# Two edge gathers: several groups summed in one PSUM run, longer rings of places and hit matrices, tile steps further apart

## The reference, cut to what matters

```python
x = x + _L0_gnn_ref(_layernorm(x), W_r, W0_w, W0_b, edge_index, edge_type_16, 6250)
x = x + _L0_ffn_ref(_layernorm(x)[None], gate_w, gate_b, w1, b1, w2, b2)[0]   # 8 experts
x = x + _L1_gnn_ref(_layernorm(x), edge_index, L1_gnn_W, L1_gnn_b)
x = x + _L1_ffn_ref(_layernorm(x)[None], W_ih, W_hh, ...)[0]                   # LSTM

# inside the first:                                       # inside the third:
msg = h_all[edge_type, src] / deg[edge_type, dst][:, None]  # norm[:, None] * h[src]
agg = segment_sum(msg, dst, num_segments=N)                 # segment_sum(..., dst, N)
```

## Time and profile before

| | us |
|---|---|
| median of the executions timed without a profile | 4071.44 (4070.2 to 4076.07) |
| span of the profiled execution | 4443.8 |
| first gather, from POOL's first gather DMA to its last | 805.7 to 1981.6 |
| second gather, likewise | 2525.9 to 3672.7 |
| POOL: busy in L941, in L1676 | 755.1, 770.6 |

### The profile page before, as it was taken

One profiled execution on the slowest core, in us unless ns is written; L12 is line 12 of the kernel. 1 busy time (PEld: TensorE's weight loads), 2 busy tenths in 40 slices (PEclk: granted clock), 3 DMA queues, 4 the chain that ended last, 5 costly groups with the idle time before them and its releaser, 6 DMA issues. The chain is left out here.

```text
span 4443.8 us, 59668 instructions
## 1 busy us (share of the span) xinstructions
PE 3422.0 (77%) x18753; PEld 2613.4 (59%) x18753; DVE 1898.4 (43%) x5881; ACT 912.0 (21%) x2407; POOL 1686.3 (38%) x1769
## 2 busy tenths in 40 slices
PE   7999999455567666667999554566667779999996
PEld 3444444354556555565666444445555557999996
DVE  4555300133334444454555421223334445544687
ACT  2333333000000111112333200000000002444554
POOL 1000000566666666653222366666666660000000
PEclk9999999677777777778999766777888889999998
DMA  4333444333444545553333323333444444433333
GB/s 148 149 149 149 154 168 164 116 107 110 124 122 144 161 134 148 150 150 108 116 113 110 109 86 94 107 116 122 126 138 146 152 154 147 153 126 119 110 109 113
DMA packets 246926, 580.34 MB, mean 131 GB/s; under 512 B 45059, under 2 KB 130588, under 8 KB 232783
## 3 DMA queue, kind: packets, MB, share of 16 engines
q1 hardware_dynamic: 158816, 334.44, 21.9%
q0 software_dynamic: 85344, 238.92, 18.3%
q10 hardware_dynamic: 2448, 3.15, 0.2%
HBM read 384.29 MB, written 191.42 MB: 130 GB/s over the span
## 5 line engine op out<-in xcount | busy, mean ns | idle before, releaser
L1676 POOL DMA_INDIRECT b_msg<-scratch_gx,k_src_row x782 | 770.6, 985 | 385.2 <-issue 220.0
L941 POOL DMA_INDIRECT a_msg<-scratch_hrel,k_rel_row x782 | 755.1, 966 | 424.1 <-issue 214.8
L717 PE MATMUL r_psm<-k_w,r_xnT 128*128 128x512 f32 x1568 | 696.4, 599 | 10.4 <-ACT k_slab L681 9.5
L1019 PE MATMUL a_ps<-a_hit,a_msg 128*128 128x128 f32 x3128 | 556.5, 343 | 170.6 <-issue 112.9
L1727 PE MATMUL b_ps<-b_hit,b_msg 128*128 128x128 f32 x3128 | 481.2, 317 | 197.3 <-issue 117.9
L1019 PEld LDWEIGHTS a_ps<-a_hit,a_msg 128*128 128x128 f32 x3128 | 501.3, 248 | 209.6 <-issue 137.4
L1727 PEld LDWEIGHTS b_ps<-b_hit,b_msg 128*128 128x128 f32 x3128 | 462.8, 230 | 246.4 <-issue 148.4
L2130 PE MATMUL l_psg<-k_hall,k_whhT 128*128 128x125 f32 x4640 | 550.7, 277 | 5.2 <-DVE k_hall L2256 5.2
L2130 PEld LDWEIGHTS l_psg<-k_hall,k_whhT 128*128 128x128 f32 x4640 | 538.4, 193 | 5.7 <-DVE k_hall L2256 5.7
L717 PEld LDWEIGHTS r_psm<-k_w,r_xnT 128*128 128x128 f32 x1568 | 294.2, 192 | 356.0 <-issue 342.5
L1831 DVE TENSOR_TENSOR k_accT<-k_accT,b_ps 128x256 f32 x196 | 82.6, 422 | 654.2 <-remote 476.0
(11 more groups left out here) (290 smaller groups left out, 4200.4 us busy)
## 6 DMA issues: line engine op xcount, KB each, us to landing
l_xr<-scratch_xrow SPq DMA_DIRECT2D x146, 512.0 KB
scratch_hrel<-k_slab SPq DMA_DIRECT2D x50, 1024.0 KB
scratch_hrel<-r_hst SPq DMA_DIRECT2D x48, 1024.0 KB
scratch_xrow<-n_xs SPq DMA_DIRECT2D x50, 512.0 KB
a_typ<-scratch_typ SPq DMA_DIRECT2D x196, 96.0 KB
a_msg<-scratch_hrel,k_rel_row POOLq DMA_INDIRECT x782
b_msg<-scratch_gx,k_src_row POOLq DMA_INDIRECT x782
n_xb<-scratch_gx SPq DMA_DIRECT2D x48, 256.0 KB
```

Source lines behind the costliest of these rows:

```text
L717: mm = pe.matmul(psm[:, c % 4], xnT[:, u, kk], k.w[:, kk, c * 512:(c + 1) * 512], start=(kk == 0), stop=(kk == 1))
L941: pool.indirect_dma_start(msg[:, q, j], None, table, bass.IndirectOffsetOnAxis(ap=rows_of[:, g, j:j + 1].bitcast(U32), axis=0)).then_inc(s ...
L1019: mm = pe.matmul(ps[:, u, kk, 0:WIN], msg[:, g % SL, j, kk * P:(kk + 1) * P], hit[:, u, j], start=(j == 0), stop=(j == pieces(g)[-1]))
L1676: pool.indirect_dma_start(msg[:, q, j], None, rows_of, bass.IndirectOffsetOnAxis(ap=k.src_row[:, g, j:j + 1].bitcast(U32), axis=0)).then_i ...
```

## The change

1. `run_regions` cuts the groups into runs of 4, 3, 2 or 1, the longest whose expected targets span at most 112 of the 128 window columns: groups 0 to 83 in fours, 84 to 113 in threes, 114 to 169 in twos, 170 to 195 alone, in all 85 runs. All groups of a run get the base of its first group (`stage_edges`, three small copies on DVE). PE adds up a whole run in PSUM, and DVE adds it to `accT` once: 85 adds in place of 196 in each gather.
2. `hit` has 4 buffers (first gather) and 6 (second). The one-hot types have 4. The ring of places has 8 and 12, the latter with four of them in `k.slab`, which is free by then.
3. `hit` is built 2 groups ahead (first) and 4 ahead (second), in place of 1. `weigh` runs 3 ahead in place of 1.
4. Each place has one landing semaphore for its four DMAs in place of four. The matmul loop has pieces outside and halves inside.
5. Tiles begin 2 slots later, and their steps stand further apart: `project` 6 and 7 slots after the beginning in place of 3 and 4, and so on. The loop has 9 slots after the last tile has begun in place of 5 (14 in place of 10 in the first gather).

```diff
-                        pe.wait_ge(s_dv, 2)
+                        pe.wait_ge(s_dv, 2 + sum(1 for _, _, m in k.regions if m > 1))
...
+                for a, z, m in k.regions:
+                    if m > 1:
+                        run = base_f[:, a:z].rearrange("o (n m) -> o n m", m=m)
+                        link(v.tensor_copy(run[:, :, 1:m], run[:, :, 0:1].broadcast_to([1, (z - a) // m, m - 1])))
...
-    SL, XR, SR, XN = 7, 4, 16, 16
+    SL, XR, SR, XN = 8, 4, 16, 16
+    HB, HT = 4, 4
...
-            begin = [k.ready[t] if along else t for t in range(NT)]
+            begin = [k.ready[t] + 2 if along else t for t in range(NT)]
...
-            slots = range(begin[-1] + 11)
+            slots = range(begin[-1] + 15)
+            landed = lambda g: 16 * sum(len(pieces(h)) for h in range(g % SL, g + 1, SL))
...
                     if along:
-                        types(0)
-                        types(1)
+                        for g in range(5):
+                            types(g)
...
                     for g in slots:
-                        if along and g + 1 < NG:
-                            weigh(g + 1)
+                        if along and g + 3 < NG:
+                            weigh(g + 3)
...
-    SL, XR, XB = 7, 4, 6
+    SL, XR, XB = 12, 4, 6
+    HB = 6
...
-        msg = sb("b_msg", [P, SL, PER, D])
-        hit = sb("b_hit", [P, 2, PER, WIN])
+        low, high = k.slab[:].rearrange("p (s j d) -> p s j d", j=PER, d=D), sb("b_msg", [P, SL - 4, PER, D])
+        msg = lambda q, j: low[:, q, j] if q < 4 else high[:, q - 4, j]
+        hit = sb("b_hit", [P, HB, PER, WIN])
...
-            first = [k.ready[t] if along else t for t in range(NT)]
+            first = [k.ready[t] + 2 if along else t for t in range(NT)]
...
-            slots = range(first[-1] + 6)
+            slots = range(first[-1] + 10)
...
                     def sums(g):
-                        u = g % 2
+                        n = k.run_of[g]
+                        begins, closes = g in k.leads, g + 1 in k.leads or g + 1 == NG
                         pe.wait_ge(s_p, g + 1)
-                        if g >= 2:
-                            pe.wait_ge(s_add, g - 1)
+                        if begins and n >= 2:
+                            pe.wait_ge(s_add, n - 1)
+                        pe.wait_ge(s_m[g % SL], landed(g))
                         for j in pieces(g):
-                            pe.wait_ge(s_m[g % SL][j], 16 * (g // SL + 1))
-                        for kk in range(2):
-                            for j in pieces(g):
-                                mm = pe.matmul(ps[:, u, kk, 0:WIN], msg[:, g % SL, j, kk * P:(kk + 1) * P],
-                                               hit[:, u, j], start=(j == 0), stop=(j == pieces(g)[-1]))
+                            for kk in range(2):
+                                mm = pe.matmul(ps[:, n % 2, kk, 0:WIN], msg(g % SL, j)[:, kk * P:(kk + 1) * P],
+                                               hit[:, g % HB, j], start=(begins and j == 0 and kk == 0),
+                                               stop=(closes and j == pieces(g)[-1]), skip_group_check=True)
                         mm.then_inc(s_mm, 1)
...
-                        for t in ahead(g, 2):
+                        for t in ahead(g, 3):
                             turn_own(t)
+                        for t in begun(g - 7):
+                            project(t, 1)
+                        for t in begun(g - 6):
+                            project(t, 0)
                         for t in begun(g - 4):
-                            project(t, 1)
-                        for t in begun(g - 3):
-                            project(t, 0)
-                        for t in begun(g - 2):
                             turn(t)
...
-                        if along and g + 1 < NG:
-                            build(g + 1)
+                        if along and g + 4 < NG:
+                            build(g + 4)
...
-                        if along and g < NG:
-                            add(g)
+                        if along and (g in k.leads[1:] or g == NG):
+                            add(g - 1)
```

More of the change, by code:

```diff
@@ L773, in stage_first @@
     s_t = (s_t0, s_t1)
-    s_m = [[k.pool_dma_sem(f"a_m{u}{j}") for j in range(PER)] for u in range(SL)]
+    s_m = [k.pool_dma_sem(f"a_m{u}") for u in range(SL)]
     nm = ("tok", "ld", "x0", "x1", "x2", "x3", "tp", "a", "st", "var", "std", "rec", "nm", "xn", "t2", "xt", "lg",
@@ L896, in sums @@
                         rest(k, pe, s_add, g + 1)
[L897 to L898 removed]
+                        rest(k, pe, s_m[q % SCAN], 16 * PER * (2 * i + q // SCAN + 1))
                         for kk in range(2):
                             for j in range(PER):
[L901 removed]
+                                mm = pe.matmul(ps[:, u, kk, 0:WIN], msg[:, q % SCAN, j, kk * P:(kk + 1) * P],
                                                hit[:, u, j], start=(j == 0), stop=(j == PER - 1))
@@ L1266, in _ @@
                     if along:
-                        hot(0)
-                        hot(1)
+                        for g in range(4):
+                            hot(g)
                         build(0)
+                        build(1)
                     v.wait_ge(S["tok"], 3)
@@ L1571, in stage_second @@
     pieces = lambda g: range(min(PER, -(-(k.E - g * EG) // P)))
-    s_m = [[k.pool_dma_sem(f"{name}m{u}{j}") for j in range(PER)] for u in range(SL)]
+    s_m = [k.pool_dma_sem(f"{name}m{u}") for u in range(SL)]
     halves = lambda a: a.rearrange("p (k c) -> p k c", k=2)
@@ L1823, in add @@
                     def add(g):
+                        n = k.run_of[g]
                         at = v.value_load(k.base[0:1, g:g + 1], min_val=0, max_val=k.NP - WIN)
                         v.wait_ge(s_mm, g + 1)
-                        if g:
-                            v.wait_ge(s_add, g)
-                        owned = sum(1 for t in range(NT) if max(first[t] - 1, 0) <= g)
+                        if n:
+                            v.wait_ge(s_add, n)
+                        owned = sum(1 for t in range(NT) if max(first[t] - 1, 0) <= g + 1)
                         if owned:
@@ L1874, in _ @@
                     if along:
-                        build(0)
+                        for g in range(4):
+                            build(g)
                     for n in range(16):
@@ L2316, in stage_lstm, with run_regions @@
         nc.all_engine_barrier()
+def run_regions(k):
+    span = lambda g, m: k.N * (((g + m) * EG / k.E) ** 2 - (g * EG / k.E) ** 2)
+    sizes, g = [], 0
+    while g < k.NG:
+        m = max([1] + [m for m in range(2, LONGEST + 1) if g + m <= k.NG and span(g, m) <= WIN - 16])
+        sizes.append((g, m))
+        g += m
+    regions = []
+    for g, m in sizes:
+        if regions and regions[-1][2] == m:
+            regions[-1] = (regions[-1][0], g + m, m)
+        else:
+            regions.append((g, g + m, m))
+    return regions
 def gnn_moe_gcn_lstm(nc, x, src, dst, edge_type_16, L0_gnn_W_r, L0_gnn_W0_w, L0_gnn_W0_b, L0_ffn_gate_w,
@@ L2338, in gnn_moe_gcn_lstm @@
     assert k.C * k.L == k.NP and k.N % k.L == 0
-    k.settled = [max(0, int(k.N * (g * EG / k.E) ** 2) - WIN // 2) // P for g in range(k.NG)]
+    k.regions = run_regions(k)
+    k.leads = [g for a, z, m in k.regions for g in range(a, z, m)]
+    k.run_of = [sum(1 for a in k.leads if a <= g) - 1 for g in range(k.NG)]
+    lead = lambda g: k.leads[k.run_of[g]]
+    k.settled = [max(0, int(k.N * (lead(g) * EG / k.E) ** 2) - WIN // 2) // P for g in range(k.NG)]
     k.ready = [next((g for g in range(k.NG) if k.settled[g] > t), k.NG) for t in range(k.NT)]
```

193 lines of the change are left out of this document (97 added, 96 removed).

## The result

The changed kernel takes **4106.9 us** (median of 4 executions, 4099.76 to 4108.0), the kernel before beside it 4073.8 (4 executions, 4070.2 to 4076.1). The ratio is 1.0078 with a 95% interval of 1.0064 to 1.0093: slower by 33 us (0.8%), well outside the 8 us that can't be told from no change. The profiled execution of the changed kernel is its fastest one: it took 4099.8 us, 7 less than the median, so its trace can show some 25 of the 33 us. The forecast of 4066 and the range up to 4090 were both too low.

A forecast was written before the change was run, and what follows sets the result against it. POOL's issue of gather DMAs was taken as the bound. Terms of -20 (waits gained), +9.4, +1.0 and +4 (tails) and +0.7 (edge-stage copies) made -5 us on the 4071.4 median: 4066, range 3975 to 4090.

The forecast's parts named there:

- What bounds the kernel: In both gathers POOL's issue of 782 indirect DMAs, 1.259 us each, is the bound, with its waits on top.
- The runs without a profile have almost none of POOL's waits: In the gathers, POOL's 321 us of profiled waits for PE are mostly absent from timed runs; 24 us taken.
- W = S - 6: W: POOL's gather waits in unprofiled runs, at least 0; S: what other stages are shorter by there, 0 to 110 us.
- S = 30: Stages outside POOL's issuing taken as 30 us shorter without a profile, leaving 24 us of POOL's waits.
- Of W's 24 us I take 20 as gained: In the gathers, all parts of the change together remove 20 us of POOL's waits; bounds 0 and 321.
- Rival 1: Slower: no POOL waits to remove, later projections stick out behind the last DMA; price 15 us, 4087; chance 0.25.
- the tails: Work behind each gather's last DMA, from steps further apart: 9.4 + 1.0 us second gather, 4 us first; bounds 0 and 20.
- beside POOL: 0: In each gather, 111 fewer adds save 47 us of DVE, but this lies beside POOL, so 0 us.
- The second tail: Behind the second gather: 12 projections left in place of 7, 9.4 us, and one more `weighted`, 1.0 us.
- The first tail: Behind the first gather: one more tile begins after the last group, 4 us.
- Rival 3: Late PE signals are in timed runs too; larger rings remove 138 us and half of 183: 3857; chance 0.08.
- What would show it: Second-gather waits far below 138 us, 85 adds per gather, slow transposes, 12 projections in a row, LSTM stretch about 10 us longer.

The follow-up runs named there:

- second profile: The kernel before, unchanged, profiled once more: 4074.8 us, with a profiled span of 4073.0 us where the earlier profile had 4443.8.
- experiment 8: Changed kernel with tile steps and beginnings at old distances, runs of one group and each add in its own slot: 4072.5 us, ratio to before 1.0006.
- experiment 10: Kernel before with the change's later beginnings and step distances in the second gather only: 4086.3 us, ratio 1.0040.
- experiment 13: Kernel before with the change's distances in the second gather only, but `turn_own` back at 2 slots ahead of a tile's begin: 4080.6 us, ratio 1.0026.
- experiment 14: Kernel before with only the first gather's tiles beginning 2 slots later, steps at old distances from the begin: 4079.7 us, ratio 1.0017.
- experiment 9: Kernel before with only the first gather's batch routing steps at the change's later distances: 4075.0 us, ratio 1.0007.
- experiment 2: Changed kernel with tile steps and beginnings back at old distances in both gathers; rings, buffers and runs of groups stay: 4091.2 us, ratio to before 1.0049.
- experiment 3: Kernel before with only the change's tile step distances and later beginnings, in both gathers: 4108.2 us, ratio 1.0083.

## Why the prediction was wrong, point by point

- **What bounds the kernel: right.** It is POOL's issue, 1.26 us a DMA. POOL's gaps are 0.3 us each, in before and after.
- **"The runs without a profile have almost none of POOL's waits": right, and sharper than it was put.** The account W = S - 6 left a door open with S = 30. There is no W at all in the second profile. S is about nothing: the three stages outside take 806.8, 484.7 and 725.7 us in the second profile and the same within 1.1 us in the first. The stretches behind POOL take 58 us where the first profile had 103; these 45 us are the lags of 46 that the account had taken off. The 6 us that it came out too high lie in POOL, 997 + 1000 us in place of 994 + 1010. **The first step that failed is S = 30, so W = 24, and with it "Of W's 24 us I take 20 as gained".** There were none to gain, and the rings, buffers and semaphores gain nothing that can be measured (experiment 8). Rival 1 named this as the point of decision, W below 7 us, and was the right case; its price of 15 us, 4087, was too low by 20 all the same, because it took the tails from the same sum. **The second step that failed is the tails, 14.4 us in the sum and 30 in the trace**; the two points on the tails say which part of each.
- **The adds, "beside POOL: 0": right in kind, not in size.** 111 adds fewer bring nothing. But the add's place, one slot later, was not priced at all. With the steps near it costs 8 to 13 us; with the steps far the whole change is no slower than the distances alone (33.1 us and 33.9). Whether the runs of groups cost anything beside that isn't shown.
- **The second tail: mechanism right, term too small.** There are 12 projections for 7, as counted. The term was 10.4 us, 16.3 were measured: the stop at `turn_own` with its lower clock (4.9 us, experiments 10 and 13) was missed. The prediction followed `project` and `weighted` past the last group, but not the step that moved the other way, from 2 slots ahead of a tile's begin to 3. The 1.0 us for a `weighted` had no row; the traces have 1.03.
- **The first tail: a whole part missed.** The sum had one more tile, 4 us. The stretch grew by 13.6, and the part missed is a batch of routing, 8 us of DVE, that came behind the slots that POOL covers. For the tiles themselves the trace leaves 5.0 us, and experiment 14, the begin alone, 2.3: the size is about right and not pinned down. The routing alone lengthens the stretch by 5.7 us (experiment 9), the begin alone by 7.1, of which some 4.8 are again the routing. The prediction costed tile steps only and never placed the batch steps in slots. It would have taken one line: the last batch but one ends in slot 183, and 185 + 11 = 196 lies behind the last group.
- **Rival 3**, with the rule of the Trainium skill on the 6.2 us ("Runtime: NRT & Kernel Launch", section "The ~15µs preamble/postamble breakdown"): the 372 us of the first profile were not in the timed executions. The page speaks of a profile's total, which the profiles here don't give, so its 6.2 us can't be tested. The spans that they do give are 1.8 us below the same execution's time in the second profile (4073.0 and 4074.8) and 1.9 in after (4097.9 and 4099.8). As a rule that a profile's waits are those of the timed executions it would have been wrong by 372 us for the first profile.
- **What would show it:** short gaps, 85 adds, 12 projections and a longer stretch to the LSTM all came. The short gaps prove nothing for the rings, since the second profile of before has them too. The slow transposes didn't come: two copies take 0.85 us with 0.36 us between, in after as in before. The time lay outside the range because the two tails cost 30 us where the sum had 14, and the gain of 20 isn't there. (The chances left out of the range add up to 0.18, not 0.19.) The 0.7 us for three copies in the edge stage has no run of its own; the stretch up to the first gather didn't grow.

## What to carry to other kernels

Where one engine bounds a stage, as POOL does here, other work moved later is covered only up to the bounding engine's last instruction; here most of what fell behind it came on top. So count, slot by slot, everything that a change pushes past that instruction, the rare batch steps and the steps moved earlier as well. A profiled execution that is some per cent longer than the timed ones isn't a picture of them: take its waits as its own until a second profile shows them too. Where engines run hand-written orders, the place of one instruction counts at the end of a stage: one add a slot later cost 8 to 13 us here, one transpose a slot earlier 4.9.

## What the runs showed that was not expected

- One profiled execution had PE's signals late, up to 17 us in the second gather, and 321 us of POOL's waits over both gathers; the same kernel profiled again had none. No run here shows what disturbed it.
- After a stop of 3.64 us PE's granted clock was 0.62 for 3.2 us (after) and a projection of 1.88 us took 3.13 and 3.43 us (after, experiment 10). After a stop of 0.63 us it was 1.00 in the 3.7 us behind (experiment 13: two projections in 3.60).
- POOL's busy time for the second gather's 782 DMAs ranges from 759.7 us (experiment 10) to 771.7 (experiment 2), with gaps that stay the same. Two kernels with the same code in that gather have 759.7 and 766.5 (experiments 10 and 3), so some 7 of the 12 us come without any difference there. What makes it longer was not tried by itself and stays open.
